# Weight splits inside the first image, a last image that ends in two halves, and a stacked group in the small network

## The reference, cut to what matters

```python
x = x + conv(_ln_c(x), Wq, bq, Wk, bk, Wv, bv, Wo, bo)     # attention over 1024 tokens, 8 heads of 64
t = _to_tokens(x)
t = t + ffn(_ln_t(t), Wa, ba, Ws, bs)                      # per token
# ffn: a few channels of a token are decoded (thresholds, first hit of 16) into 8 x 160 features,
# of which only the first two positions count; y_add and y_sub are two networks of three layers
#   h = W[i] h + b[i], 160 -> 160 -> 160 -> 160, relu after the first two
# two outputs (100 and 101) of the network that the token's marks select are rounded,
# and 33 channels of the token are changed by them
```

## Time and profile before

| what | before |
|---|---|
| median of 3 runs | 2641.2 us (2638.88 to 2643.03) |
| the profiled execution | 2638.7 us, its span 2636.9 us |
| granted TensorE clock, mean | 0.989 |
| busy share PE, DVE, ACT, POOL | 95%, 72%, 65%, 34% |
| first matmul, last store issued | 31.6 us, 2632 us |

### The profile page before, as it was taken

The page is one execution under the profiler, slowest core; times in us unless marked ns, Lnnn a source line. Parts: engine busy times, 40 slices in busy tenths (PEclk is TensorE's granted clock), DMA queues, the critical chain, the costliest instruction groups (busy, mean ns, idle before and its releaser), DMA issues.

```text
span 2636.9 us, 37209 instructions
## 1 busy us (share of the span) xinstructions
PE 2510.1 (95%) x13344; PEld 2053.7 (78%) x13344; DVE 1909.7 (72%) x3507; ACT 1721.2 (65%) x3048; POOL 890.0 (34%) x804
## 2 busy tenths in 40 slices
PE   4999999999999999999999999999999999999986
PEld 3788777887788777887778878788787887778874
DVE  4677767777677776778767786677867777677763
ACT  3677547775477755777367773677736776477753
POOL 0244403444144431444314433144422444134430
PEclk9999999999999999999999999999999999999997
DMA  6222313232033411234123331232412223123310
GB/s 253 62 73 63 140 33 87 70 111 102 17 92 84 128 65 48 80 77 132 49 65 77 76 124 45 76 75 67 151 33 69 76 69 140 33 81 76 83 50 32
DMA packets 79941, 215.14 MB, mean 82 GB/s; under 512 B 9968, under 2 KB 10256, under 8 KB 74000
## 3 DMA queue, kind: packets, MB, share of 16 engines
q1 hardware_dynamic: 79760, 212.77, 26.9%
HBM read 103.68 MB, written 25.17 MB: 49 GB/s over the span
## 4 chain that ended last, share of the span: by engine, by line
PE 79%; DVE 11%; ACT 5%; issue 2%; POOL 1%; DMA 1%; SPq 0%; ACTq 0%; DVEq 0%
PE pT L486 14%; PE pJ L452 10%; PE pO L501 9%; PE pO L502 9%; PE pS L473 7%; PE pS L474 7%; PE pa L549 5%; PE po L625 5%; PE pv L598 5%; PE pv L452 2%; DVE PL L834 2%; ACT PH L716 2%; ACT PR L685 1%; DVE b_stats L996 1%; DVE nmax L805 1%
## 5 line engine op out<-in xcount | busy, mean ns | idle before, releaser
L409 POOL TENSOR_SCALAR PR<-PR,rinv 128x1024 f32<-128x1024 f32 x512 | 575.3, 1124 | 1237.0 <-DVE rinv L809 1237.0
L834 DVE TENSOR_TENSOR PL<-pT,PH 128x512 fp32r<-128x512 f32 x1024 | 658.5, 684 | 326.4 <-ACT PH L716 324.5
L716 ACT ACTIVATE PH<-pT 128x512 fp32r<-128x512 f32 x1024 | 557.4, 598 | 359.9 <-PE pT L486 348.0
L805 DVE TENSOR_REDUCE nmax<-pS 128x1 f32<-128x1024 f32 x512 | 622.5, 1216 | 33.7 <-PE pS L474 25.6
L685 ACT ACTIVATE PR<-pS,nmax 128x1024 f32<-128x1024 f32 x512 | 574.7, 1123 | 4.7 <-DVE nmax L805 1.5
L486 PEld LDWEIGHTS pT<-ident,PR 128*128 128x128 f32 x4096 | 475.4, 141 | 99.8 <-POOL PR L409 37.5
L486 PE MATMUL pT<-ident,PR 128*128 128x128 f32 x4096 | 534.6, 273 | 12.7 <-POOL PR L409 10.6
L501 PE MATMUL pO<-PH,VS 128*128 128x512 f32 x1024 | 410.3, 401 | 14.6 <-DVE OT L825 14.6
L473 PE MATMUL pS<-KHL,QS 128*128 128x512 f32 x1024 | 415.7, 406 | 4.6 <-ACT PR L685 2.2
L502 PE MATMUL pO<-PL,VS 128*128 128x512 f32 x1024 | 406.8, 397 | 0.0
L474 PE MATMUL pS<-KHL,QS 128*128 128x512 f32 x1024 | 402.2, 393 | 0.0
(11 more groups left out here) (151 smaller groups left out, 3023.1 us busy)
## 6 DMA issues: line engine op xcount, KB each, us to landing
KHL<-HL SPq DMA_DIRECT2D x192, 256.0 KB, 3.6
X<-in_x SPq DMA_DIRECT2D x64, 512.0 KB, 6.9
WQ<-wqk_split SPq DMA_DIRECT2D x64, 512.0 KB, 4.3
QS<-HL SPq DMA_DIRECT2D x192, 128.0 KB, 3.0
WO<-wo_split SPq DMA_DIRECT2D x16, 1024.0 KB, 7.3
out<-X SPq DMA_DIRECT2D x16, 1024.0 KB, 4.3
KHL<-wv_split SPq DMA_DIRECT2D x14, 1024.0 KB, 8.9
KHL<-KHL SPq DMA_DIRECT2D x16, 512.0 KB, 4.2
```

The costliest lines, as they stand in the source:

```text
L409: pool.tensor_scalar(PR[g % 2][:, :], PR[g % 2][:, :], M["rinv"][:, g:g + 1], 1.0, ALU.mult, ALU.mult)\
L716: act.activation(PH[ck % 2][:, 4 * half:4 * half + 4, (g % 4) * P:(g % 4 + 1) * P], pT[half][:, :].rearrange("p (k n) -> p k n", k=4), ACT ...
L805: dve.tensor_reduce(nmax[:, g:g + 1], pS[g % 2][:, :], AX.X, ALU.max, negate=True).then_inc(S["a_max"], 1)
L834: dve.tensor_tensor(PL[ck % 2][:, ks, qs], pT[half][:, :].rearrange("p (k n) -> p k n", k=4), f32(PH[ck % 2][:, ks, qs]), ALU.subtract).th ...
```

## The change

1. The setup block is gone. Its loads are issued by SP at the head of `sync_program`, the identity and image 0 first; the splits are items W0 to W5 of ACT and DVE inside image 0's front, the query and key halves apart, and the buffers lie where later buffers do. Heads 0 and 1 of image 0 take their weights by a copy within SBUF.
2. `EDGES` becomes `START` (image 0's front), `EDGE` (between images, new orders) and `LAST` (image 7). In `LAST` the tokens are two halves of 512: S, F, L, Y, results and R run for the first half while the second is still on its way (S10 to S15 and S20 to S25; the columns of F, L and Y are sorted so that quarters 0 and 1 belong to the first half).
3. The short group of layer 1 is stacked: high and low weight of its 64 columns stand side by side as one 128-column tile `W1T`, which multiplies H1H and H1L, six matmuls instead of nine. The two halves of the result are added afterwards (HTOP on ACT, HSUM on DVE), and its own high and low part are stacked along the rows of `H2T`, so that layer 2 is three matmuls instead of four.
4. In the attention steps the 16 value matmuls of a block stand as four in each step, those of g%4 = 0 behind the turn; the fetch of their sum moves from step g%4 = 0 to g%4 = 3.

```diff
-            with nc.Block() as block:            # the setup block, lines 155 to 218
...
+    sp.dma_start(*setup["ident"]).then_inc(S["ident_in"], 16)
+    for t in range(CT):
+        sp.dma_start(M["X"][:, t, :], dram["x"][0, :, t, :]).then_inc(S["f_x"], 16)
+    sp.dma_start(*setup["wv"]).then_inc(S["wv_in"], 16)
+    sp.dma_start(*setup["wqk"]).then_inc(S["wqk_in"], 16)
...
+    sp.wait_ge(S["lo_o"], 1)
+    for k, half in enumerate(("woh", "wol")):
+        sp.dma_start(dram["wo"][:, k, :], f32(M[half][:, :, :].rearrange("p k n -> p (k n)"))).then_inc(S["wo_out"], 16)
     sp.wait_ge(S["wqk_out"], 32)
...
+START = {
+    "scalar": """W0 T0 T1 T2 T3 T4 T5 T6 T7 N0 B0 B1 W2 B2 V0 W1 V1 B3 W3 B4 V2 V3 B5 B6 B7 W5 V4 V5 V6 V7 Q0 Q1 Q2 Q3
...
+LAST = {
+    "tensor": """E65 E66 E67 O0 O1 O2 O3 O4 O5 O6 U0 U1 U2 U3 O7 U4 U5 U6 U7 F0 F1 L0 L10 F2 F3 L1 L20 L11 L2 L21 L3 L12
+        Y10 L22 L13 R0 R1 R2 L23 R3 Y20 R4 R5 R6 R7""",
...
-        if g >= 4 and g % 4 > 0:
+        if 4 <= g < STEPS and g % 4 > 0:
+            values(i, g // 4 - 1, 2 * (g % 4), 2 * (g % 4) + 2)
+        elif STEPS < g < STEPS + 4:
             values(i, g // 4 - 1, *((0, 3), (3, 6), (6, 8))[g % 4 - 1])
         if 0 <= g < STEPS:
             turn(i, g)
+            if g >= 4 and g % 4 == 0:
+                values(i, g // 4 - 1, 0, 2)
...
+            rows = [P, P, 2 * TAIL + 2]
+            for k, K in enumerate(rows):
+                wait("b_h1lo", i, 3 * q + k + 1)
+                w = W1T[0:K, k, :, :].rearrange("p a b -> p (a b)")
+                pe.matmul(pa[1][:, :], w, H1H[q % 2][0:K, k, :], start=(k == 0), stop=False)
+                mm = pe.matmul(pa[1][:, :], w, H1L[q % 2][0:K, k, :], start=False, stop=(k == 2))
...
+            pe.matmul(py[:, :], W2S[:, 1, :], H2T[:, :], start=True, stop=False)
+            pe.matmul(py[:, :], W2S[:, 0, :], H2H[:, :], start=False, stop=False)
+            pe.matmul(py[:, :], W2S[:, 0, :], H2L[:, :], start=False, stop=True).then_inc(S["b_l2"], 1)
...
# ACT, second layer of quarter q
+            act.activation(M["HTOP"][:, :], pa[1][D:P, :], ACT.Copy).then_inc(S["b_h2top"], 1)
+            wait("b_h2sum", i, q + 1)
...
+            act.activation(M["H2T"][0:D, :], M["HSUM"][:, :], ACT.Relu).then_inc(S["b_h2hi"], 1)
...
# ACT and DVE, fetching the sum of a block
-        if g >= 8 and g % 4 == 0:
-            ck = g // 4 - 2
+        if g >= 7 and g % 4 == 3:
+            ck = g // 4 - 1
...
# DVE, second layer of quarter q
+            dve.tensor_tensor(M["HSUM"][:, :], pa[1][0:D, :], M["HTOP"][:, :], ALU.add).then_inc(S["b_h2sum"], 1)
...
+            dve.scalar_tensor_tensor(out=M["H2T"][D:P, :], in0=M["HSUM"][:, :], scalar=0.0, in1=f32(M["H2T"][0:D, :]),
+                                     op0=ALU.max, op1=ALU.subtract).then_inc(S["b_h2lo"], 1)
```

More of the change, by code:

```diff
@@ L303, in schedule, with halves @@
-    return order
+        order += [("A", i, g) for g in range(4, 64)] + work(EDGE if i + 1 < N_IMG else LAST, i)
+    return order
+def halves(ap, k):
+    return ap.rearrange("p (a b) -> p a b", b=P)[:, :, k * D:(k + 1) * D]
 def split_qk(dve, bank, QSb, KHb, KLb, bias, n):
@@ L877, in vector_program, with select @@
         "Y8", "Y4", "YS", "YR", "EQ", "CY"))
-    def select(i):
-        for s in range(ST):
+    def select(i, n):
+        sl = part(n)
+        for s in range(sl.start, sl.stop):
             last = dve.tensor_scalar(XN[:, s, :], X1[:, 0, s * P:s * P + SEL], r[:, s:s + 1], nb[:, s:s + 1],
@@ L883, in select, with nibbles @@
         last.then_inc(S["b_sel"], 1)
-        wait("b_sel", i, 1)
-    def nibbles(i):
-        group = above[:, :, :].rearrange("p s (g k) -> p (s g) k", k=16)
-        step(dve.tensor_scalar(above[:, :, :], XN[:, :, 16:80], 0.5, None, ALU.is_gt))
-        step(dve.tensor_tensor(group, group, M["ramp"][:, :].unsqueeze(1).to_broadcast([P, ST * 4, 16]),
+        wait("b_sel", i, 2 if n > 20 else 1)
+    def nibbles(i, n):
+        sl = part(n)
+        rows = sl.stop - sl.start
+        group = above[:, sl, :].rearrange("p s (g k) -> p (s g) k", k=16)
+        step(dve.tensor_scalar(above[:, sl, :], XN[:, sl, 16:80], 0.5, None, ALU.is_gt))
+        step(dve.tensor_tensor(group, group, M["ramp"][:, :].unsqueeze(1).to_broadcast([P, rows * 4, 16]),
@@ new lines, in nibbles, with features @@
+        step(dve.tensor_scalar(tmp, flat, -1.0, 16.0, ALU.mult, ALU.add))
+        step(dve.scalar_tensor_tensor(out=flat, in0=flat, scalar=0.5, in1=tmp, op0=ALU.is_gt, op1=ALU.mult))
+    def features(i, n):
+        sl = part(n)
+        rows = sl.stop - sl.start
+        step(dve.tensor_scalar(cmp3[:, sl, :], XN[:, sl, 0:3], 0.5, None, ALU.is_gt))
+        dve.tensor_tensor(mask[:, sl, 0], cmp3[:, sl, 0], cmp3[:, sl, 1], ALU.mult)
+        dve.tensor_tensor(mtmp[:, sl, 0], cmp3[:, sl, 0], cmp3[:, sl, 2], ALU.mult)
+        dve.tensor_copy(XNR[:, sl, :], XN[:, sl, 105:107])
+        step(dve.tensor_scalar(mtmp[:, sl, 1], cmp3[:, sl, 1], -1.0, 1.0, ALU.mult, ALU.add))
+        step(dve.tensor_tensor(mask[:, sl, 1], mtmp[:, sl, 0], mtmp[:, sl, 1], ALU.mult))
+        dve.tensor_tensor(active[:, sl], mask[:, sl, 0], mask[:, sl, 1], ALU.add)
+        dve.tensor_tensor(XNL[:, sl, :], XN[:, sl, 105:107], f32(XNR[:, sl, :]), ALU.subtract)
@@ L997, in vector_program @@
         elif kind == "S":
-            if n == 0:
-                statistics(i, "b", 1e-5)
-            elif n == 5:
-                scales(i, "b")
-                step(dve.tensor_scalar(M["r1"][:, :], M["b_r"][:, :], 1.0, None, ALU.add))
+            if n % 10 == 0:
+                statistics(i, "b", 1e-5, n)
+            elif n % 10 == 5:
+                scales(i, "b", n)
+                step(dve.tensor_scalar(M["r1"][:, part(n)], M["b_r"][:, part(n)], 1.0, None, ALU.add))
             else:
-                (select, nibbles, features, results)[n - 1](i)
+                (select, nibbles, features, results)[n % 10 - 1](i, n)
         elif kind == "L" and n < 10:
```

505 lines of the change are left out of this document (273 added, 232 removed).

## The result

The changed kernel takes 2578.2 us (median of 4 executions, 2575.3 to 2580.17) against 2642.11 for the kernel before on the same chip: ratio 0.9755, 95% interval 0.9735 to 0.9775, so 2.5% faster. The forecast was 2560 with a range of 2541 to 2588. Direction and range hold. But the range was that wide because it took in the rivals; the forecast's own range, 2546 to 2574, is missed by 4 us, and of the 79 us of the sum 58.5 came. The span of the profiled execution went from 2636.9 to 2578.4, its time is 2580.17.

What follows compares the result with a forecast made beforehand. PE, busy 95% of the span, was taken as the bound: its work plus its waits. Gains 18 + 34.5 + 5.5 + 9 + 12 = 79 from 2638.7 gave 2559.7, forecast 2560; own range 2546 to 2574, with rivals 2541 to 2588.

Steps and rivals of the forecast that it cites:

- Front: Image 0 before attention: first token copy 20.1 us earlier, less 2.3 for wv's subtraction; gain 18 us (12 to 22).
- the subtraction of wv: Image 0's front, DVE behind the scales: it and POOL's tiles hold each other up, costing the full 2.3 us.
- The other splits: Query, key and wo weight splits on ACT and DVE in image 0: cost nothing, up to 4 us.
- Stacked group: Small network's layers 1 and 2, images 0 to 6: fewer matmuls save 4.9 us per image, 34.5 for seven.
- edge orders: Between images: new orders take 0.8 us per image of PE's 3.9 idle; gain 5.5 us for seven (0 to 14).
- Attention steps: Steps without projection: new value spread removes the sum's wait, adds one behind it; half taken, gain 9 us (-10 to +19).
- Image 7: Last image's tail: features of half 0 earlier, result tiles and store halved; gain 12 us (6 to 17), stacked matmuls included.
- The network's chain: Rival: small network's ACT and DVE chain stalls PE about 1.0 us per quarter, costing 28 us, 2588; chance 0.10.
- The turn held up by the fetch: Rival, attention blocks: fetch delays the step's copies; 175 us fully shown (2744, chance 0.02), 17 at a tenth (2586, 0.06).

Runs made afterwards that it cites:

- e5: The changed kernel with DVE's subtraction of wv ahead of image 0's token subtractions instead of behind the scales; 2575.61 us, ratio 0.9755 to the kernel before.
- e6: The changed kernel with the old orders between images put back, stacked group and new fetch kept; 2593.64 us, ratio 0.9813 to the kernel before.
- e2: The changed kernel with the old spread of the value matmuls (6, 6 and 4) and the fetch one step later; 2579.99 us, ratio 0.9771.
- e9: The changed kernel with the last image's splits H0 and H1 ahead of the fetch of the last block's sum; 2570.74 us, ratio 0.9736.
- E67: Not a run: the item in the written orders that fetches the last block's sum, in the last image ahead of the attention result's splits H0 and H1.
- e1: The changed kernel with the short group unstacked, 18 matmuls in layer 1 and four in layer 2 per quarter; 2627.72 us, ratio 0.9951.

## Why the prediction was right, and where it was not

- **Front, 18 forecast, 17.6 measured.** By its own steps: ACT late by wv, the first token copy 19.6 us earlier, the subtraction of wv costing nearly its 2.29 in the first scale tile and low part. The other splits showed nothing in front, as was taken. No run puts the setup block back, so the 17.6 us are read from the stages, and by e5 what the subtraction costs at the end of the front isn't shown.
- **Stacked group and edge orders, 34.5 + 5.5 = 40 forecast, 36.2 measured** (41.4 in the edges once the fetch's 4.2 is set apart, less 5.2 in steps 0-4). The sum is nearly right, the division not. The stacked group's 4.9 us per image was read rightly from the matmuls (5.1 of busy time), but it needs an order that feeds it: with the old orders the edges fell by 18.3 us only (747.1 to 728.8), with the new ones by 42.2. Without the clock falls in the edges (an estimate, 1.4 to 1.6 us each) that is 24 and 39, so most of the difference is the order and not luck. The mis-sized term is the orders, 19.7 instead of 5.5: I took 0.8 us per image out of 3.9 idle. The window of the 3.9 reaches into step 0; in the edges as cut here PE idles 23.6 us in all, 3.4 each, and 11.6 after, 1.7 each (the residual's wait is gone). I gave no price to what the clock does behind such a wait, 1.4 us in five images of e6, nor to the second layer's waits that an order made for the old lengths brings. The 5.2 us lost in steps 0-4 were also not counted: some 2.8 by 0.4 us per image without a fall, of which the longer wait for the result step (1.19 instead of 0.91) is the larger part, and 2.3 by two more clock falls.
- **Attention steps, +9 forecast, about 0 in e2's comparison.** This is the step that failed. The forecast said that the spread "removes the wait for the sum and adds one behind it" and took half of 19 us as gain. The wait removed was mis-read: the sum takes the 14.6 us as 32 equal waits, a quarter of them (4) at the edges, while 8.4 stand behind the last steps (0.9 in each of seven edges and 2.2 in image 7) and only 6.2 in the steps. The wait added, 15.2 us in 24 waits, is more than twice that. The nearest rows gave the reason beforehand: the fetch costs ACT 0.69 and DVE 0.68, and ahead of the transposes of steps 52 and 60 ACT and DVE had no such slack. What kept the sum near zero is the edges (4.2) and steps 52-63, where idle time fell by 3.6 us all the same. The 0.06 us per block in the 88 blocks with projections, 5 us in all, had no row.
- **Image 7, 12 forecast, 5.2 measured.** The mechanism is right: features of half 0 come 15.95 us after the first transposes U (16.0 forecast; 17.0 before), and the undisturbed tail of e5 is 94.2, a gain of 11.0. The late start of the projection is in that 11.0: 9.92 instead of 8.74 us behind the last pT, 1.2 lost against a kernel that itself lost there (a wait of 2.2 us and value matmuls at the lower clock), and 3.4 against e9, since E67 was written ahead of H0 and H1. The other 5.8 went with the clock in the profiled execution, 3.0 in the output projection and 2.7 behind the features. e9's gain is 13.6, of which the halves make up to 6.9 and the stacked group about 5 (e1's tail is 99.2 with no fall in its output projection, e5's 94.2).
- **The rivals.** The network's chain did not become the bound: PE's waits for H2L are 1.7 us in all, against the 28 of that rival. The turn held up by the fetch was real, at 5 us in steps 48-52 and not 17 to 175; it took back a gain instead of making the kernel slower. Since no rival put together a null in the loop and half a tail, the time fell between the forecast's own range (2546 to 2574) and the end of the wide one. That the wide range holds is owed to rivals that did not happen, and is luck to that extent; the direction, the front and the stacked group's matmuls are not.

## What to carry to other kernels

An order and a shorter instruction list are not two terms that add: price the order with the new durations in it. Where a wait is moved by putting a fetch one step earlier, look at what the same engines do next on the critical chain; a fetch ahead of the copies is paid where nothing else keeps PE busy. Where a total is given over many waits, look where they stand before a share of it is taken. And compare stages cut at one recurring instruction, since they show 0.1 us where medians show 3.
